# Norm 0's rows, zero fills and late weights written or read behind the first products, degrees summed on VectorE, and 1 + eps applied where sums are added

## What is computed

```python
h = _layernorm(x)                                   # norm 0
neigh = segment_sum(h[src], dst, num_segments=n)     # 100000 edges, dst sorted
h = (1.0 + eps) * h + neigh                          # GIN sum
h = relu(h @ W1 + b1) @ W2 + b2                      # then batch norm
# attention of layer 0, beside it, on the same normed rows:
q, k, v = split(rmsnorm(h) @ w_qkv); q = softmax(q, features); k = softmax(k, nodes)
out = rmsnorm((context @ q) @ w_out + b_out) + h
# layer 1's graph convolution needs deg = segment_sum(edge_weight, dst) and the dense weights
```

## Time and profile before

| | us |
|---|---|
| runs shown | 2343.05, 2343.22, 2350.0 |
| median | 2343.22 |
| the profiled execution, its own time | 2350.05 |
| its span, first to last instruction | 2348.5 |
| PE, DVE, ACT, POOL busy in the span | 2094.3, 1723.9, 1227.1, 442.9 |
| mean granted clock of TensorE | 0.933 of full speed |

### The profile page before, as it was taken

How to read it: one execution, slowest core, us unless ns; L and a number is a source line. 1 busy time by engine, 2 the same in 40 slices (tenths; PEclk the granted TensorE clock), 3 DMA queues, 4 the chain that set the end, 5 groups by cost and what they waited for, 6 DMA issues and landing times. The chain is left out here.

```text
span 2348.5 us, 46441 instructions
## 1 busy us (share of the span) xinstructions
PE 2094.3 (89%) x17737; PEld 1948.1 (83%) x17737; DVE 1723.9 (73%) x3473; ACT 1227.1 (52%) x2856; POOL 442.9 (19%) x363
## 2 busy tenths in 40 slices
PE   4456999999856999996899999999998999999996
PEld 2246999999755999996577899989987999999996
DVE  5689787788478888885666566556656887888885
ACT  4445555555433776664551544444435225666774
POOL 4430000000004444444000000000000032444443
PEclk9677999999966999998799999999996999999998
DMA  6112333333543877776200566456642015777786
GB/s 207 48 45 69 112 88 88 112 86 91 156 151 109 225 233 232 233 222 194 58 1 24 168 188 188 143 153 188 185 137 94 20 50 166 233 222 229 224 231 167
DMA packets 236905, 338.84 MB, mean 144 GB/s; under 512 B 29305, under 2 KB 198342, under 8 KB 236550
## 3 DMA queue, kind: packets, MB, share of 16 engines
q1 hardware_dynamic: 208800, 296.14, 40.1%
q0 software_dynamic: 24432, 35.68, 8.4%
q10 hardware_dynamic: 3446, 3.97, 0.5%
HBM read 258.83 MB, written 76.90 MB: 143 GB/s over the span
## 5 line engine op out<-in xcount | busy, mean ns | idle before, releaser
L2260 PE MATMUL bank<-WB_r,XN_r 128*128 128x448 f32 x1400 | 399.7, 367 | 3.7 <-DVE WB_r L2219 3.7
L2219 DVE TENSOR_TENSOR WB_r<-WB,WB_r 128x448 fp32r<-128x448 f32 x350 | 213.9, 624 | 166.2 <-ACT WB_r L2212 166.1
L2212 ACT CAST WB_r<-WB 128x448 fp32r<-128x448 f32 x350 | 197.7, 568 | 222.2 <-PE bank L2260 217.8
L2260 PEld LDWEIGHTS bank<-WB_r,XN_r 128*128 128x128 f32 x1400 | 263.2, 188 | 26.8 <-DVE wb__r L2185 4.4
L1816 PE MATMUL bank<-SC_r,WB_r 128*128 128x256 f32 (+1 forms) x2064 | 257.5, 285 | 14.6 <-issue 12.5
L1816 PEld LDWEIGHTS bank<-SC_r,WB_r 128*128 128x128 f32 x2064 | 251.3, 193 | 19.0 <-issue 19.0
L1011 ACT CAST WB_r<-bank 128x200 fp32r<-128x200 f32 x391 | 137.4, 351 | 203.0 <-PE bank L995 201.3
L1831 PE MATMUL bank<-R_r,H_r 128*128 128x256 f32 x1752 | 215.9, 282 | 4.8 <-DVE R_r L1727 4.8
L1831 PEld LDWEIGHTS bank<-R_r,H_r 128*128 128x128 f32 x1752 | 209.7, 189 | 5.1 <-issue 5.1
L1680 ACT ACTIVATE wb_<-bank,WB 128x256 f32<-128x256 f32 (+1 forms) x344 | 133.6, 476 | 99.0 <-issue 63.5
L1816 PE MATMUL bank<-SC_r,XN_r 128*128 128x256 f32 x1392 | 171.3, 282 | 6.6 <-issue 5.9
(11 more groups left out here) (427 smaller groups left out, 5281.4 us busy)
## 6 DMA issues: line engine op xcount, KB each, us to landing
WB<-adjw SPq DMA_DIRECT2D x350, 224.0 KB, 2.9
WB<-in_f_pack SPq DMA_DIRECT2D x127, 512.0 KB
WB<-in_f_pack SPq DMA_DIRECT2D x62, 640.0 KB
adjw<-X SPq DMA_DIRECT2D x24, 1600.0 KB, 7.6
WB<-in_f_pack SPq DMA_DIRECT2D x65, 516.0 KB
xd<-XN SPq DMA_DIRECT2D x15, 640.0 KB
y<-X SPq DMA_DIRECT2D x10, 640.0 KB, 3.3
X<-y SPq DMA_DIRECT2D x6, 640.0 KB, 6.8
```

Of the source, the lines that this page charges most:

```text
L2212: e.copy(split_w(m)[0], RAW[m % PR]).then_inc(S("whigh"), 1)
L2219: e.tensor_tensor(al, RAW[m % PR], ah.bitcast(F32), ALU.subtract).then_inc(S("wlow"), 1)
L2260: mm_ = e.matmul(conv_bank(k, band, c)[:, 0:PW], x[st][:, o], y, start=(st == 0 and i == 0), stop=(st == T - 1 and i == 2))
```

## The change

Seven edits. (1) SP starts with a wait for the last first product. Then it stores XD, then zeroes the paddings, and late_sp waits for those to land, because the zero area now lies in wa, where the first late weights go. (2) The waits for the zero fills in ACT's copies and in DVE's stage 2 go, and the ones columns of v are written earlier. (3) The degrees are 26 instructions on DVE (comparison, product and sum in one, 128 columns each) behind the last turn of norm 0; POOL only masks and stores them. (4) The first three passes of senders_dve move to the same place, the last two stay. (5) The splits of edge weights are cut into single subtractions on DVE and casts on ACT, spread over the rounds; each of the four fills has its own place for the rest. (6) L1175's pass over XT goes: sums_dve multiplies with 1 + eps (scalec) as it adds. The fallback of POOL for unsorted edges keeps the pass. (7) The wait for the late weights moves from DVE's L1175 to PE's first layer1_pe, and ACT's copies of normed rows wait for the degrees' sums rather than for POOL's product.

```diff
-    HALVES = ((0, 7), (7, WG))
-    wprod = h_all[:, 3 * WN:3 * WN + 7 * 128].rearrange("p (g n) -> p g n", n=128)
+    wprod = [sc_all[:, i:i + 128] for i in range(0, 2048, 128)] + [h_all[:, i:i + 128] for i in range(3 * WN, 3 * WN + 1280, 128)]
...
     high2, mid2, low2 = keys(WB, 6400), keys(r1_all, 2528), keys(r1_all, 0)
-    left = WB[:, 6400 + WINDOWS:6400 + WINDOWS + 512]
...
+    left = [WB[:, 6400 + WINDOWS:6400 + WINDOWS + 512], h_all[:, 3 * WN:3 * WN + 512],
+            WB[:, 6400 + WINDOWS:6400 + WINDOWS + 512], r1_all[:, 1853:2365]]
...
-    zero = R1[:, 1, :]
+    zero = wa[:, :]
...
     def late_sp(e):
+        e.wait_ge(S("fill"), 16 * NF)
...
+    def weights_dve(e):
+        for g in range(WG):
+            for r in range(2):
+                e.scalar_tensor_tensor(wprod[2 * g + r], wrel[:, g, :], r - 0.5, eew[:, g, :], ALU.is_equal, ALU.mult,
+                                       accum_out=deg2[:, g, r:r + 1]).then_inc(S("fold"), 1)
     def degrees_pool(e):
-        e.wait_ge(S("inside"), 1)
-        e.wait_ge(S("edges"), 16 * WG)
-        p = Chain(e, S("fold"))
-        for g0, g1 in HALVES:
-            prod = wprod[:, 0:g1 - g0, :]
-            for r in range(2):
-                p.wait()
-                p.add(e.tensor_scalar(prod, wrel[:, g0:g1, :], r - 0.5, None, ALU.is_equal))
-                p.wait()
-                p.add(e.tensor_tensor(prod, prod, eew[:, g0:g1, :], ALU.mult))
-                for n in (64, 32, 16, 8, 4, 2):
-                    p.wait()
-                    p.add(e.tensor_tensor(prod[:, :, 0:n], prod[:, :, 0:n], prod[:, :, n:2 * n], ALU.add))
-                p.wait()
-                p.add(e.tensor_tensor(deg2[:, g0:g1, r], prod[:, :, 0], prod[:, :, 1], ALU.add))
-        p.wait()
+        e.wait_ge(S("fold"), 2 * WG)
         e.wait_ge(S("good"), 1)
         e.tensor_scalar(deg2, deg2, goodc, None, ALU.mult).then_inc(S("degrees"), 1)
...
-    def senders_dve(e, c):
-        e.wait_ge(S("edges"), 16 * WG)
+    def places_in_tiles_dve(e, c):
         c.add(e.tensor_scalar(whii.bitcast(I32), esrc, 7, None, ALU.logical_shift_right))
         c.wait()
         c.add(e.tensor_scalar(whii, whii.bitcast(I32), 1.0, None, ALU.mult))
         c.wait()
         e.scalar_tensor_tensor(wlo, whii, -128.0, esrc, ALU.mult, ALU.add).then_inc(S("wkey"), 1)
+    def tiles_dve(e, c):
...
     def highs_act(e, f):
         e.wait_ge(S("keyT"), 2 * FILLS + f + 1)
         e.copy(high2[:, windows_of(f), :], twice(part_of(f))).then_inc(S("lo16"), 1)
-    def parts_of_dve(e, c, f):
...
+        return FILLS + 4 * (f // 2) + 2 * k + f % 2 + 1
+    def act_step(f, k):
+        return FILLS + 6 * (f // 2) + 2 * k + f % 2 + 1
+    def rest_of(f):
         o = windows_of(f)
-        rest = left[:, 0:o.stop - o.start]
-        e.wait_ge(S("lo16"), FILLS + f + 1)
-        c.add(e.tensor_tensor(rest, part_of(f), high2[:, o, 0], ALU.subtract))
-        c.wait()
-        c.add(e.tensor_copy(mid2[:, o, :], twice(rest)))
-        c.wait()
-        c.add(e.tensor_tensor(rest, rest, mid2[:, o, 0], ALU.subtract))
-        c.wait()
-        e.tensor_copy(low2[:, o, :], twice(rest)).then_inc(S("key16"), 1)
+        return left[f][:, 0:o.stop - o.start]
+    def first_rest_dve(e, f):
+        e.wait_ge(S("lo16"), act_step(f, 0))
+        e.tensor_tensor(rest_of(f), part_of(f), high2[:, windows_of(f), 0], ALU.subtract).then_inc(S("key16"), 1)
+    def mids_act(e, f):
+        e.wait_ge(S("key16"), dve_step(f, 0))
+        e.copy(mid2[:, windows_of(f), :], twice(rest_of(f))).then_inc(S("lo16"), 1)
+    def second_rest_dve(e, f):
+        e.wait_ge(S("lo16"), act_step(f, 1))
+        e.tensor_tensor(rest_of(f), rest_of(f), mid2[:, windows_of(f), 0], ALU.subtract).then_inc(S("key16"), 1)
+    def lows_act(e, f):
+        e.wait_ge(S("key16"), dve_step(f, 1))
+        e.copy(low2[:, windows_of(f), :], twice(rest_of(f))).then_inc(S("lo16"), 1)
...
         e.tensor_scalar(grow, rstd, 1.0, None, ALU.add).then_inc(S("mix0_dve"), 1)
+        for section in sections:
+            c.add(e.memset(section.one(), 1.0))
+        weights_dve(e)
+        places_in_tiles_dve(e, c)
...
         e.wait_ge(S("mix0_dve"), (M0V_RS if t < 4 * RS_HALF else M0V_RS2) + 1)
-        if t == 22:
-            e.wait_ge(S("fill"), 16 * NF)
...
-            if j in TURNED[0:2]:
-                highs_act(e, TURNED.index(j))
+            if j in (1, 2):
+                highs_act(e, j - 1)
+            if j in (2, 3):
+                mids_act(e, j - 2)
+            if j in (4, 5):
+                lows_act(e, j - 4)
...
-        e.wait_ge(S("fill"), 16 * NF)
-        for section in sections:
-            c.add(e.memset(section.one(), 1.0))
...
-        senders_dve(e, c)
+        tiles_dve(e, c)
...
-            if j + 1 in TURNED[0:2]:
-                parts_of_dve(e, c, TURNED.index(j + 1))
+            if j in (0, 1):
+                first_rest_dve(e, j)
+            if j in (2, 3):
+                second_rest_dve(e, j - 2)
...
+        if o.start % 512 == 0:
+            e.wait_ge(S("lo16"), act_step(o.start // 512, 2))
...
         to = XT[:, :, 128 * b:128 * b + n]
         if b == 0:
             e.wait_ge(S("gate"), 1)
+            e.wait_ge(S("qk"), T)
+            e.wait_ge(S("xts"), 1)
         e.wait_ge(S("sT"), b + 1)
-        e.tensor_tensor(to, to, B[4 + b % 2][:, D:2 * D].rearrange("p (c n) -> p c n", c=2)[:, :, 0:n], ALU.add).then_inc(S("gadd"), 1)
+        e.scalar_tensor_tensor(to, to, scalec, B[4 + b % 2][:, D:2 * D].rearrange("p (c n) -> p c n", c=2)[:, :, 0:n],
+                               ALU.mult, ALU.add).then_inc(S("gadd"), 1)
...
-            e.wait_ge(S("key16"), 2 * FILLS)
+            e.wait_ge(S("w_late"), W_LATE)
+            e.wait_ge(S("key16"), dve_step(FILLS - 1, 0))
...
-                        e.wait_ge(S("degrees"), 1)
+                        e.wait_ge(S("fold"), 2 * WG)
                     e.copy(xnh[:, fifth(i - 1)], xn_all[:, fifth(i - 1)]).then_inc(S("xnh"), 1)
                 if (b, i) == (0, 6):
                     highs_act(e, 3)
+                if b == 1 and i in (2, 4):
+                    mids_act(e, 1 + i // 2)
+                if (b, i) in ((1, 6), (2, 0)):
+                    lows_act(e, b + 1)
                 if i == 0 and 2 <= b < T + 2:
...
     def count_dve(e, d):
-        d.add(e.tensor_scalar(epsc, epsc, 1.0, None, ALU.add))
-        d.wait()
+        e.tensor_scalar(scalec, epsc, goodc, 1.0, ALU.mult, ALU.add).then_inc(S("xts"), 1)
...
-                if (b, i) == (0, 2):
-                    e.wait_ge(S("qk"), T)
-                    e.wait_ge(S("w_late"), W_LATE)
-                    e.tensor_scalar(XT[:, :, :], XT[:, :, :], epsc, None, ALU.mult).then_inc(S("xts"), 1)
...
-                if b == 1 and i in (4, 6):
-                    parts_of_dve(e, d, i // 2)
+                if b == 1 and i in (1, 3):
+                    first_rest_dve(e, 2 + i // 2)
+                if b == 1 and i in (5, 7):
+                    second_rest_dve(e, i // 2)
                 if i == 3 and 2 <= b < T + 2:
...
         early_sp(e)
-        e.wait_ge(S("x_in1"), 32)
+        e.wait_ge(S("qk"), T)
+        store_sp(e, XD, XN, "xd_out", xn_ready(e, 0))
         zero_sp(e)
-        store_sp(e, XD, XN, "xd_out", xn_ready(e, 0))
         late_sp(e)
```

More of the change, by code:

```diff
@@ L129, in program @@
     b1c, b2c, gac, bec = cols[:, 0:4], cols[:, 4:6], cols[:, 6:8], cols[:, 8:10]
-    gprec, gb1, gb2, epsc = cols[:, 10:12], cols[:, 12:14], cols[:, 14:16], cols[:, 16:17]
+    gprec, gb1, gb2, epsc, scalec = cols[:, 10:12], cols[:, 12:14], cols[:, 14:16], cols[:, 16:17], cols[:, 17:18]
     rows = sb("rows", [128, 3 * D + 8])
@@ L407, in turn_weights_pe @@
             e.wait_ge(S("edges"), 16 * WG)
-        e.wait_ge(S("key16"), f + 3)
+        if f < 2:
+            e.wait_ge(S("key16"), f + 3)
+        else:
+            e.wait_ge(S("key16"), dve_step(f - 2, 0))
         turn_keys_pe(e, eew, f, 6 + f % 2).then_inc(S("keyT"), 1)
@@ L413, in highs_act, with dve_step @@
         e.copy(high2[:, windows_of(f), :], twice(part_of(f))).then_inc(S("lo16"), 1)
-    def parts_of_dve(e, c, f):
-        o = windows_of(f)
-        rest = left[:, 0:o.stop - o.start]
-        e.wait_ge(S("lo16"), FILLS + f + 1)
-        c.add(e.tensor_tensor(rest, part_of(f), high2[:, o, 0], ALU.subtract))
-        c.wait()
-        c.add(e.tensor_copy(mid2[:, o, :], twice(rest)))
-        c.wait()
-        c.add(e.tensor_tensor(rest, rest, mid2[:, o, 0], ALU.subtract))
-        c.wait()
-        e.tensor_copy(low2[:, o, :], twice(rest)).then_inc(S("key16"), 1)
+    def dve_step(f, k):
+        return FILLS + 4 * (f // 2) + 2 * k + f % 2 + 1
+    def act_step(f, k):
+        return FILLS + 6 * (f // 2) + 2 * k + f % 2 + 1
+    def rest_of(f):
+        o = windows_of(f)
+        return left[f][:, 0:o.stop - o.start]
[11 more added lines that the diff above has]
+        e.copy(low2[:, windows_of(f), :], twice(rest_of(f))).then_inc(S("lo16"), 1)
```

(5 more changed lines are left out.)

## The result

The changed kernel takes 2331.20 us in the median (2326.16 to 2336.19, five executions) against 2344.51 of before (2343.05 to 2350.0, five): a ratio of 0.9948, 95% interval 0.9933 to 0.9962, 13.3 us less. The forecast was 2331.3. That the median falls within 0.1 us of the forecast is luck in part: before came out 1.3 us above the 2343.2 that the forecast started from, and the change returned 1.4 more than the 11.9 of its sum. The two profiled executions differ by more, 2350.05 against 2331.2, 18.85 us. That the total came out is therefore no proof of the terms, and most of the runs went into this gap.

A forecast was written before the change was run, and what follows sets the result against it. DVE's program was taken as the path from 86 to about 215 us, then PE. Terms 1.0 + 2.2 + 3.0 + 3.5 + 2.2 = 11.9 us took the median from 2343.2 to 2331.3; range 2318 to 2342.

The forecast's parts named there:

- the hold: In norm 0, group 4: PE's turns modelled to end at 56.4, copies start at 62.2; 5.8 us with a product unannounced.
- norm 0, up to T: Start to the last turn's copy on DVE: SP's fills and stores leave, 1.0 us less; bounds 0 and 9.
- stage 2: Behind the last turn's copy: POOL's sums leave, 26 combined DVE instructions are added; 2.2 us less, range nothing to 4.3.
- stage 3: Two fills: DVE loses two casts each, ACT takes four; 3.0 us less, or 0 if ACT's roots come late.
- blocks 0 and 1: L1175's 3.55 us pass goes, 3.5 less in block 0; DVE loses 1.8 of casts, 2.2 less in block 1.
- the longer hold: In norm 0 at group 4: given to POOL's gathers, which stay, because SP issues nothing there; 5.8 us.
- rival A: Norm 0: the holds go with the stores, 8.0 us more, 19.9 in all, 2323.3; chance 0.27.
- Contention 9.3: Stage 2: DVE instructions took longer beside POOL's sums than alone, together 9.3 us.
- PE's context: End of stage 2: 6.59 us for 22 of 25 tiles, so 7.5 for all.
- both paths: Stage 2: DVE alone and the path over ACT and PE each give 2.2 us and arrive together.
- B: Stages 2 and 3: ACT becomes the bound, only 5.7 us returned, 2337.5; chance 0.17.
- C: Behind the last turn: holds travel with the stores, 18.8 us of holds, net 7.9 slower, 2351.1; chance 0.06.

The follow-up runs named there:

- e4: The kernel before, unchanged, profiled a third time, on the third chip: 2344.99 us (one execution).
- a2: The changed kernel, unchanged, run a third time, on the third chip: 2329.43 us, 0.9951 of before.
- the second block: Four runs on a second chip: the changed kernel again, two reorderings of it, and the kernel before with the SP move alone; before took 2342.98 us there.
- s2: Changed kernel with the 26 additions in DVE's idle time before the last turn's copy and three sender passes back behind k's subtractions: 2323.34 us, 0.9919 of before.
- e5: Changed kernel with SP's old order (fills, stores, late weights early), run again on the third chip: 2333.07 us, 0.9955 of before.
- a1: The changed kernel, unchanged, run again on the second chip: 2328.97 us, 0.9949 of before.
- e2: Changed kernel with only the five stores of normed rows back at their old early place, first chip: 2339.26 us, 0.9948 of before.
- e3: Changed kernel with only the seven zero fills back at their old early place, first chip: 2337.86 us, 0.9952 of before.
- m1: Kernel before with the SP part alone: stores, fills and late weights behind the last first product; second chip: 2341.34 us, 0.9995 of before.
- e0: The kernel before, unchanged, profiled once more on the first chip: 2345.57 us (one execution).
- s1: Changed kernel with its 26 additions moved into DVE's idle time before the last turn's copy, second chip: 2326.31 us, 0.9927 of before.
- s3: s2 with ACT's copies no longer waiting for DVE's places and more DVE work in norm 0's waits, third chip: 2319.59 us, 0.9901 of before.

## Why the prediction was right, step by step

The fair pair for the terms is e4 and a2: same chip, neither with the hold. T is the start of the last turn's copy here; the prediction counts from about its end, 86.0.

| step | forecast | e4 to a2 |
|---|---|---|
| norm 0, up to T | -1.0 | 77.39 to 77.49: +0.1 |
| stage 2, T to the readout (L896, L915) | -2.2 | 49.93 to 48.48: -1.45 |
| readout to the first mixed tile | none | 12.99 to 11.92: -1.07 |
| stage 3 | -3.0 | 27.96 to 24.79: -3.17 |
| blocks 0 and 1, to the first sum | -5.7 | 48.78 to 43.25: -5.53 |
| the further sums | 0 | 403.99 to 405.04: +1.05 |
| together | -11.9 | -10.1 |

The medians fell by 13.0 here, 14.0 in the second block and 13.3 in the first pair, the means of the first two by 11.5 and 12.4. Ahead of the last sum the traces give 10.1; the rest lies behind the counting, where single executions scatter too much to tell 3 us: from the last sum to the end the profiled executions take 1713.1 us (s2) to 1728.9 (e5), and a1 and after, the same kernel, 1716.2 and 1719.7.

*Norm 0.* The size came out near (1.0 forecast; +0.1 in the trace, 1.1 of mean in time), and it was luck that it did. The step "I therefore give the longer hold to the gathers, which stay" has the right partner as far as the runs show: where the hold exists, it stayed with the stores away and with the fills away (e2, e3), and it ended with the gathers' traffic. What the step missed is that gathers alone don't make it: on the other chips gathers, stores and fills run together without it (e4, e5). No run took the gathers away, so the cause stays open. The forecast's sign that "DVE's and ACT's copies of group 4 still at about 61" failed in every profile of the changed kernel, and rival A's "if they come at 55, A is right" would have convicted the stores and fills without proof: the copies came at 57.1, but so they do with stores and fills early on the third chip (56.9 in e5), and the total of A (2323.3) didn't come. The page of the Trainium skill that the prediction names, "SBUF — State Buffer", section "SBUF: two separate sides", says that transfers can't slow an engine's work; on the chips without the hold the trace agrees (+0.1 at T between e4 and a2, and DVE's prices in m1 within 0.1 us of those without transfers). Whether the hold on the first chip goes against it isn't shown.

*Stage 2.* The terms held but for two. Contention 9.3: before's readout stands 49.9 us behind the turn's copy, that of s2, with the same DVE work, no POOL beside it and no additions, 40.3, so 9.6 (the single prices were less exact: L341 clean is 2.39, not 1.93, L345 2.40, not 1.95). Additions 7.1: 26 at one per 0.25 us, 6.5. DVE alone is thus 3.1 shorter and not 2.2. The second exponential was to come 10.2 us later against T and came 10.5 later. The term that missed is PE's context, "6.59 for 22 of 25 tiles, so 7.5": the same 44 products took 7.51 and the last six 1.03, 8.5 in all. They ran at a granted clock of 0.78 in the first profile and of 0.67 in the changed kernel:

```profile
117.60:124.20 6.60, 6.60 (x47) 6.60 (x47) 6.50 (x4) 4.64 (x10) 6.44 (x3) 0.78 0.00 0
```

```profile
116.30:123.80 7.50, 7.50 (x47) 7.50 (x47) 6.59 (x9) 4.64 (x10) 0.37 (x1) 0.67 0.80 230
```

The change isn't what made them slower. The kernel before took 7.97 us for them in e0 and 8.11 in e4, at 0.62:

```profile
109.30:117.40 8.10, 8.10 (x47) 8.08 (x47) 8.00 (x4) 4.65 (x10) 7.86 (x4) 0.62 0.00 0
```

The 6.59 of the earlier trace rows is the shortest of all fourteen profiles. In each of them PE had worked little just ahead, at a granted clock of 0.50 (1.01 of 9.25 us in the kernel before, 1.49 in the changed one), and they differ in how soon the clock rose again. A clock-bound term taken from one execution carries such a scatter, 6.6 to 8.1 us. So the path over ACT and PE ends the stage: DVE waits 1.69 us for it (1.83 in a2), and the term is 1.45, not 2.2. That both paths lay close was seen; that the additions should then not stand ahead of ACT's first exponential was not.

*Readout to the first mixed tile.* Not in the sum, and no accident: 12.99 us in all three profiles of the kernel before, 11.92 or 11.93 in all three of the changed one. PE had stood 9.43 us for DVE's readout in e4 and ran the stretch at a granted clock of 0.80; in a2 it had stood 0.65 and ran at 1.00. With the wait on PE's side gone, this 1.07 makes up for the 1.0 of norm 0 that the trace doesn't show.

*Stages 3 and 4.* Right to 0.2 us each. ACT's casts took 1.045 us against the 1.0 assumed, its roots weren't late, and the pass of 3.55 us is gone whole. "A few hundredths per block" for the multiplication is what the further sums may show: L1099 takes 0.48 us where L1074 took 0.42, and 24 sums later the counting is 1.05 us behind. No run shows that the one makes the other.

*The rivals.* B would have needed ACT as the bound in stage 3; it is busy 18.95 of 25.5 us there. C needed holds behind the last turn. None is seen: behind the last turn no wait up to the readout is put down to "remote", in the changed kernel or in e2 and e3 on the chip with the hold.

## What to carry to other kernels

A wait in one profile can belong to the chip, or to the session, and not to the kernel. Before a term is built on a wait whose releaser is "remote" or that no program order explains, profile the same kernel again on another chip; a pair of profiles from two chips can differ by more than the change. When work is moved onto an engine, look for its existing waits first: the 26 additions cost 6.5 us at the head of a stage, and nothing in the 8.8 us for which the same engine waited just before. A wait that one engine loses can turn up on the next, and then cost clock: look at what PE does just ahead of a stretch that it bounds. And check each wait's count against the order in which the signals really come: behind one that is too high by one ACT stood 3.5 us and PE 4.4 (in s2).

## What the runs showed of the hardware

- On one chip, and in the profile shown before the prediction, PE's signals of group 4 come 5 to 7 us after the modelled end of its products, with copies at 62.0 to 62.4 in all five profiles; on the two other chips in none of eight, with copies at 56.2 to 57.7. The kernel before takes 9 to 10 us longer there by its means, 6 to 7 at one clock. The hold ends less than 0.8 us after the traffic of POOL's gathers, but the gathers run in all fourteen profiles, so what makes it wasn't found.
- Beside POOL's sums DVE's instructions with two inputs take 0.6 us more at 1408 columns, 0.3 to 1.8 more at 1664 (1.8 is L341) and 1.0 to 1.9 more at 384; one with a single input and 1664 columns takes 0.5 more (1.03 to 1.53), the integer shift of 1664 columns 1.27 us either way. Transfers at 135 to 140 GB/s beside DVE leave all of them alone.
- A combined instruction with an accumulated sum is issued every 0.25 us at 128 columns, although the profile gives 0.33 for itself and 0.09 for its readout: the busy times overlap.
- The stretch behind the readout has the same 65 products in all profiles. Where PE had stood 0.65 us before it (a1, s1, a2) it takes 11.9 us at a granted clock of 1.00, whether the readout came at 126.0 or at 118.1; where PE had stood 3.31 us (s2), 3.57 (s3) or 9.43 (e4), 12.8 us at 0.87, 13.6 at 0.75 and 13.0 at 0.80.
